# The middle row of a per-channel 7 by 7 convolution goes from VectorE to TensorE

## Chip, core and metric

The kernel runs on one core of a Trainium2 chip. The metric is the device time of one execution in microseconds (us); lower is better. Five engines run at the same time and wait for one another by semaphores: TensorE (PE in the rows, PEld for its weight loads) multiplies matrices, VectorE (DVE) and GpSimd (POOL) work elementwise, ScalarE (ACT) applies functions and copies, SyncE (SP) starts transfers.

## What is computed

16 images of 256 channels and 32 by 32 points pass through two layers. Both start with a group normalisation and add their result to their input.

```python
# layer A, one image x (256, 32, 32), xh = groupnorm(x)
key = softmax_over_points(K_w @ xh + K_b)                      # 49 x 1024
f   = xh @ key.T                                               # 256 x 49
w   = conv1_w @ relu(layernorm(conv0_w @ f + b0)) + b1         # 7 x 7 taps for each channel
x   = x + depthwise_conv7x7(xh, w)                             # each channel with its own 49 taps
...
# layer B: projections to 128 channels at three resolutions (1024, 256, 64 points),
# 16-state scans forwards and backwards over them, layernorm, upsampling, gate, projection
h = h * exp(delta * A) + delta * B * x ;  y += C * h
x = x + out_w @ (y * silu(z))
```

## The kernel before

A channel sits on a partition, so an image is 2 tiles (`CT`, index `t`) of 128 partitions by 1024 points. Three images are in flight: in one pass of `body(i, j, m)` image i is in the scans of layer B, image j in the convolution of layer A, and image m has its taps made (normalisation, softmax, the small matrices). `stages` writes that pass for each engine: 37 **units** (`NU`), then a **bridge** between two images. Every engine has its own order of instructions, written out by hand, and meets the others through counting semaphores only.

- There are five passes in the program text: one with image m alone, one with j and m (the **head**, in which no scan runs), a loop of 14 with all three, one with i and j (its units hold a convolution too, its bridge no work for an image m), one with i alone. Units with both scans and a convolution are thus run for 15 images, bridges with all three for 14; 13 of these jump back to the start of the loop (L1363).
- Units 0 to 4 hold the coarse levels of the scan, units 5 to 36 one state each at 1024 points. In such a unit VectorE runs `scan` (L553), `weigh` (L563, or L566 in the coarse units) and `inputs` of the unit after it (L531). TensorE spreads one row of B over 128 partitions into the PSUM tensor `slot_b` (`put_b`, L850) once the scan has freed it, and one row of C into `slot_c` (`put_c`) once `weigh` has. `inputs` of unit k+1 needs `put_b(k+1)`, and `weigh` overlaps it. ScalarE makes the decays (L1136), GpSimd adds each product to `y` (`gather`, L1268).
- Small steps for image m (`pre`, for example `gn_spread` in unit 6, `a_spread_` in 23, `a_f3_` in 25, `a_w_` in 26), the normalisations of y (`norm`) and `conv_add` stand between them on VectorE. I call them **fillers**; a scan waits behind them in VectorE's order.
- The convolution on TensorE: a tap is a matmul with a diagonal 128 by 128 matrix (`diag`) over the shifted image, in three float16 products and two halves, so 6 matmuls of 512 columns (L799, `taps`), all into `pconv`. `taps_at` deals the taps to the units 0 to 32 by the weights `ROOM`; in a unit they stand behind `put_c`. In the bridge 7 taps of the next image stand between other matmuls.
- The diagonals of a row of 7 taps are made on GpSimd by two instructions (`make_row`, L1245), in a ring of 4 rows; `row_unit` derives from `taps_at` in which unit a row is made, behind that unit's `gather`.
- Row 3 of 7, the **middle row**, is not on TensorE: `middle_taps` runs its 14 taps (7 of each of the two tiles) on VectorE in the bridge, one instruction a tap (L465 the first of a tile, which adds `xr`; L471 the others), into `xm`, which lies in `u`. The first 7 stand ahead of `chunk_first` (L494), the last 3 just ahead of `inputs(j, 0)`. `copy_x` (L1046) copies `xm` to `xn`, to which `conv_add` (L479) adds the TensorE part.

The bridge has a chain over three engines: TensorE's projection of image j (L807), its lower levels (L825), the first chunk (L839, L840), `chunk_first` on VectorE, the second chunk on TensorE, the normalisation of image i (L880, L886), taps, a projection (L816), the output of image i (L893), taps, `put_b(j, 0)`, and at last `inputs(j, 0)`.

Of the kernel before, what the change touches and what calls it, by code (L numbers as in the profile page):

```python
# [62 lines left out]
def build(nc, a, out):  # L63
    with ExitStack() as ctx:  # L64
# [79 lines left out]
        wmid = sb("wmid", [P, CT, KK])  # L144
# [22 lines left out]

        xm = u[:, 0:CT * HW].rearrange("p (t n) -> p t n", t=CT)
# [28 lines left out]
        ea_a, ea_b = Chain("dve_a", 19), Chain("dve_b", 3)  # L197
# [27 lines left out]
        mid_tap = Count("mid_tap", len(MID_TAPS))  # L225
# [110 lines left out]
        def _(dve):  # L336
# [106 lines left out]
            def a_w_(j):  # L443
# [177 lines left out]
            def bridge(i, j, m):  # L621
                def some(lo, hi):
                    if m is not None:
                        middle_taps(m, BRIDGE_MID[lo], BRIDGE_MID[hi])
# [793 lines left out]
```

## Time and profile before

| | us |
|---|---|
| median of 3 runs | 4960.43 (4957.82 to 4961.94) |
| the profiled execution | 4965.09 |
| its span, from the first to the last instruction | 4963.0 |
| VectorE busy | 4530.2 |
| TensorE matmuls busy | 3601.6 |
| GpSimd busy | 3041.7 |
| ScalarE busy | 1639.2 |

The mean granted TensorE clock was 0.852 of full speed. The spans of instructions on one engine may overlap slightly, since the next one starts while the last one drains.

### The profile page before, as it was taken

Reading aid. Unit: us, or ns where it says so; the run is one execution under the profiler, and the core shown is the slowest. Engines: PE = TensorE matmul, PEld = TensorE weight load, DVE = VectorE, ACT = ScalarE, POOL = GpSimd, SP = SyncE. Lnnn points to the kernel's source line nnn. Section 1 sums busy time; section 2 is a strip of 40 time slices with the busy share of each in tenths; the row PEclk is TensorE's granted clock in tenths of the full one; section 3 lists DMA queues with packets and bytes.
Section 4 is the critical chain, followed back from the end, with each engine's and each line's share of the span. In section 5 each row is a group of like instructions: output and inputs, shape, how many; then the busy total and the mean of one; then the engine's idle time right before and its main releaser. Section 6 shows DMA issues by size and latency. Waiting matters only on the chain. (4 is left out here: it accounts for less than half of the span.)

```text
span 4963.0 us, 44208 instructions
## 1 busy us (share of the span) xinstructions
PE 3601.6 (73%) x14156; PEld 1531.7 (31%) x14156; DVE 4530.2 (91%) x3880; ACT 1639.2 (33%) x2518; POOL 3041.7 (61%) x1748
## 2 busy tenths in 40 slices
PE   6877786777868777786777867778676777867744
PEld 3423332333323223332233323333232333322210
DVE  4499999999998999999999999999999999999898
ACT  1232334323333333333324233233333323342332
POOL 3375756757566575755757566575765757557474
PEclk8988888888988888888888888888888888888855
DMA  1000000000000000000000000000000000000000
GB/s 35 9 1 0 18 1 18 0 0 18 1 18 0 9 9 0 18 0 18 1 0 18 1 18 0 0 18 1 18 0 17 1 0 18 1 9 1 9 0 9
DMA packets 11799, 38.96 MB, mean 8 GB/s; under 512 B 1680, under 2 KB 2848, under 8 KB 11552
## 3 DMA queue, kind: packets, MB, share of 16 engines
q1 hardware_dynamic: 11552, 35.70, 2.0%
q8 instruction: 151, 2.47, 0.2%
q14 instruction: 96, 0.79, 0.1%
HBM read 18.92 MB, written 16.78 MB: 7 GB/s over the span
## 5 line engine op out<-in xcount | busy, mean ns | idle before, releaser
L799 PE MATMUL pconv<-pad,diag 128*128 128x512 f16 x8064 | 2114.1, 416 | 49.6 <-DVE xn L479 38.4
L1268 POOL TENSOR_TENSOR y<-y,work 128x1024 f32<-128x1024 f32 (+2 forms) x672 | 1332.6, 1983 | 1220.9 <-DVE work L563 1202.7
L1136 ACT ACTIVATE work<-delta,nega 128x1024 f32<-128x1024 f32 (+1 forms) x768 | 696.5, 931 | 2282.5 <-DVE work L553 2060.5
L799 PEld LDWEIGHTS pconv<-pad,diag 128*128 128x128 f16 x8064 | 835.7, 104 | 1225.2 <-issue 351.3
L553 DVE TENSOR_TENSOR_SCAN work<-work,slot_b 128x1024 f32<-128x1024 f32 x496 | 1132.0, 2282 | 23.2 <-issue 3.2
L850 PE MATMUL slot_b<-bcs,sel 96*128 96x512 bf16 (+2 forms) x1536 | 431.3, 388 | 782.4 <-DVE work L553 536.6
L531 DVE TENSOR_TENSOR slot_b<-slot_b,u 128x1024 f32<-128x1024 f32 x496 | 607.6, 1225 | 164.9 <-PE slot_b L850 145.3
L563 DVE TENSOR_TENSOR work<-slot_c,work 128x1024 f32<-128x1024 f32 x512 | 626.9, 1224 | 22.0 <-DVE work L553 0.5
L1263 POOL TENSOR_TENSOR work<-work 128x512 f32<-128x512 f32 (+3 forms) x384 | 549.4, 1431 | 134.7 <-DVE work L566 117.2
L850 PE MATMUL slot_c<-bcs,sel 96*128 96x512 bf16 (+2 forms) x1536 | 417.1, 376 | 292.2 <-DVE work L563 199.9
L1245 POOL TENSOR_TENSOR diag<-id,chi 128x896 f16<-128x896 f16 x192 | 378.9, 1974 | 248.1 <-DVE csc L384 180.0
L850 PEld LDWEIGHTS slot_b<-bcs,sel 96*128 96x128 bf16 x1536 | 108.7, 105 | 1036.2 <-DVE work L553 712.9
L553 DVE TENSOR_TENSOR_SCAN work<-work 128x1028 f32<-128x1028 f32 x144 | 393.2, 2730 | 2.0 <-POOL y L1268 0.2
L1245 POOL TENSOR_TENSOR diag<-id,clo 128x896 f16<-128x896 f16 x192 | 370.0, 1927 | 0.0
L471 DVE SCALAR_TENSOR_TENSOR u<-xh,wmid,u 128x992 f32<-128x992 f32 (+2 forms) x192 | 307.4, 1655 | 0.0
L850 PEld LDWEIGHTS slot_c<-bcs,sel 96*128 96x128 bf16 x1536 | 100.7, 101 | 607.0 <-DVE work L563 452.2
L1224 POOL TENSOR_TENSOR bcs<-rest,bcs 32x512 bf16<-32x512 f32 (+1 forms) x96 | 165.7, 1726 | 187.6 <-ACT bcs L1108 187.6
L566 DVE TENSOR_TENSOR work<-slot_c,work 128x1024 f32<-128x1024 f32 x160 | 195.0, 1219 | 7.8 <-PE slot_c L850 3.8
L1227 POOL TENSOR_TENSOR delta<-delta,rs 128x512 f32<-128x512 f32 (+1 forms) x96 | 99.0, 1031 | 102.0 <-DVE rs L509 102.0
L1231 POOL TENSOR_TENSOR u<-delta,f 128x512 f32<-128x512 f32 (+1 forms) x96 | 135.4, 1411 | 8.6 <-POOL delta L1227 2.2
L839 PE MATMUL pm<-f,wbc 128*96 128x512 f32 (+1 forms) x192 | 101.7, 616 | 37.0 <-DVE rest L494 29.8
L1093 ACT ACTIVATE bcs<-pm 96x512 bf16<-96x512 f32 (+1 forms) x96 | 46.9, 488 | 170.2 <-PE pm L839 170.2
(177 smaller groups left out, 3693.2 us busy)
## 6 DMA issues: line engine op xcount, KB each, us to landing
xr<-in_x SPq DMA_DIRECT2D x16, 1024.0 KB, 4.8
out<-ob SPq DMA_DIRECT2D x16, 1024.0 KB
w<-in_w SPq DMA_DIRECT2D x2, 256.0 KB
wc<-in_wc SPq DMA_DIRECT2D x2, 256.0 KB
wbc<-in_wbc SPq DMA_DIRECT2D x1, 144.0 KB
win<-in_win SPq DMA_DIRECT2D x1, 128.0 KB
wz<-in_wz SPq DMA_DIRECT2D x1, 128.0 KB
wo<-in_wo SPq DMA_DIRECT2D x1, 128.0 KB
```

What stands on the lines that cost most here:

```text
L471: ins = nc.vector.scalar_tensor_tensor(o, src, w, o, ALU.mult, ALU.add)
L531: nc.vector.tensor_tensor(o, i0, i1, ALU.mult).then_inc(u_bx.sem, 1)
L553: nc.vector.tensor_tensor_scan(hv, av, bv, 0.0, ALU.mult, ALU.add).then_inc(q_h.sem, 1)
L563: nc.vector.tensor_tensor(hv, slot_c[:, :], hv, ALU.mult).then_inc(q_pr.sem, 1)
L566: nc.vector.tensor_tensor(hv, slot_c[:, :].rearrange("p (m l) -> p m l", m=m), hv, ALU.mult).then_inc(q_pr.sem, 1)
L799: ins = nc.tensor.matmul(bank(pconv, k), w, pad[:, t, part, rows:rows + 16, dx:dx + W], start=first and m == 0, stop=last and m == 2)
L850: ins = nc.tensor.matmul(slot[:, o:o + per], sel[:, row0 + n0 + n:row0 + n0 + n + 1].to_broadcast([96, P]), bcs[:, so + c:so + c + per], s ...
L1136: ins = nc.scalar.activation(o, delta[:, so:so + ln], ACT.Exp, scale=nega[:, st, n0 + n:n0 + n + 1])
L1224: pool.tensor_tensor(bcs[0:32, s:s + n], rest[0:32, c % 2, 0:n], bcs[0:32, s:s + n], ALU.subtract).then_inc(ch_lo.sem, 1)
L1245: ins = pool.tensor_tensor(diag[:, r % RING, m, :, :], id16[:, None, :].to_broadcast([P, KK, P]), w[:, t, dy * KK:(dy + 1) * KK, None].to_ ...
L1263: pool.tensor_tensor(src[:, 0:m], src[:, 0:m], src[:, m:2 * m], ALU.add).then_inc(n_y.sem, 1)
L1268: pool.tensor_tensor(yv, yv, src[:, 0] if len(src.shape) == 3 else src, ALU.add).then_inc(q_y.sem, 1)
```

## The change

All 7 rows of both tiles are dealt to TensorE. `ROWS` has 14 rows in place of 12, so that TensorE has 98 taps an image in place of 84 and GpSimd makes 14 rows of diagonals in place of 12. `middle_taps`, its semaphore, the copy `wmid` in `a_w_` and the waits of ScalarE and GpSimd for `xm` are gone; `copy_x` reads `xr` itself. The 7 taps of TensorE in the bridge stay, so that its units get 89 in place of 75. One weight of `ROOM` goes from -28 to -27.

```diff
-MIDDLE = KK // 2
-ROWS = [(t, r) for t in range(CT) for r in range(KK) if r != MIDDLE]
+ROWS = [(t, r) for t in range(CT) for r in range(KK)]
-MID_TAPS = [(dx, t) for dx in sorted(range(KK), key=lambda d: abs(d - MIDDLE)) for t in range(CT)]
...
-                ch(nc.vector.tensor_copy(wmid[:, :, :], wg[:, :, MIDDLE * KK:(MIDDLE + 1) * KK]))
...
-            def middle_taps(j, lo, hi):
-                for n in range(lo, hi):
-                    dx, t = MID_TAPS[n]
-                    shift = dx - MIDDLE
-                    w = wmid[:, t, dx:dx + 1]
-                    if shift == 0:
-                        ins = nc.vector.scalar_tensor_tensor(xm[:, t, :], xh[:, t, :], w, xr[:, t, :], ALU.mult, ALU.add)
-                    else:
...
-                        ins = nc.vector.scalar_tensor_tensor(o, src, w, o, ALU.mult, ALU.add)
-                    ins.then_inc(mid_tap.sem, 1)
...
             def bridge(i, j, m):
-                def some(lo, hi):
-                    if m is not None:
-                        middle_taps(m, BRIDGE_MID[lo], BRIDGE_MID[hi])
-                some(0, 1)
...
-                act.wait_ge(mid_tap.sem, mid_tap.at(j + 1, 0))
-                nc.scalar.activation(xn[:, :, :], xm[:, :, :], ACT.Copy).then_inc(a_copy.sem, 1)
+                nc.scalar.activation(xn[:, :, :], xr[:, :, :], ACT.Copy).then_inc(a_copy.sem, 1)
...
-                if c == 2 and j is not None:
-                    pool.wait_ge(a_copy.sem, a_copy.at(j, 1))
...
-BRIDGE_MID = (0, 7, 10, 11, 11, 14)
...
-for k, v in {0: -16, 1: 8, 2: 4, 3: 14, 4: 4, 6: 6, 10: 0, 11: -8, 13: -10, 14: -8, 15: -28, 16: -10, 17: -12, 19: -4, 20: -10, 22: 3, 23: 7,
+for k, v in {0: -16, 1: 8, 2: 4, 3: 14, 4: 4, 6: 6, 10: 0, 11: -8, 13: -10, 14: -8, 15: -27, 16: -10, 17: -12, 19: -4, 20: -10, 22: 3, 23: 7,
```

The weights deal the taps anew. The units 0, 2, 3, 4, 6, 8, 10, 13, 16, 17, 19, 22, 24, 26, 27, 29 and 31 get one tap more, the units 14, 18 and 28 one fewer. Three places show what stands where. In these rows the line numbers of the changed kernel are its own: its L766 is L799 before, L817 is L850, L1209 is L1245, L1232 is L1268, L508 is L531.

VectorE at the end of the bridge of the loop, before, from the last output instruction to the jump back:

```order
L617 SCALAR_TENSOR_TENSOR ob<-slot_b,vec,xc 128x512
L468 REGISTER_ALU
L471 SCALAR_TENSOR_TENSOR u<-xh,wmid,u 128x32x29
L468 REGISTER_ALU
L471 SCALAR_TENSOR_TENSOR u<-xh,wmid,u 128x32x29
L468 REGISTER_ALU
L471 SCALAR_TENSOR_TENSOR u<-xh,wmid,u 128x32x29
L520 ISA
L531 TENSOR_TENSOR b<-slot_b,u 128x16x64
L1363 REGISTER_ALU
L1363 COMPARE_AND_BRANCH
```

And in the changed kernel:

```order
L594 SCALAR_TENSOR_TENSOR ob<-slot_b,vec,xc 128x512
L497 ISA
L508 TENSOR_TENSOR b<-slot_b,u 128x16x64
L1326 REGISTER_ALU
L1326 COMPARE_AND_BRANCH
```

Nothing stands between the output and `inputs(j, 0)` any more; the other 11 middle taps are gone from their places in the same way.

TensorE from `put_b(5)` in unit 3 to `put_b(6)` in unit 5, before:

```order
L850 MATMUL slot_b<-bcs,sel 128x512 x2
L786 REGISTER_ALU
L799 MATMUL pconv<-pad,diag 128x512 x12
L865 REGISTER_ALU
L850 MATMUL slot_c<-bcs,sel 128x256 x4
L799 MATMUL pconv<-pad,diag 128x512 x30
L865 REGISTER_ALU
L850 MATMUL slot_c<-bcs,sel 128x512 x2
L786 REGISTER_ALU
L799 MATMUL pconv<-pad,diag 128x512 x12
L858 REGISTER_ALU
L850 MATMUL slot_b<-bcs,sel 128x512 x2
```

And in the changed kernel:

```order
L817 MATMUL slot_b<-bcs,sel 128x512 x2
L766 MATMUL pconv<-pad,diag 128x512 x12
L832 REGISTER_ALU
L817 MATMUL slot_c<-bcs,sel 128x256 x4
L766 MATMUL pconv<-pad,diag 128x512 x18
L753 REGISTER_ALU
L766 MATMUL pconv<-pad,diag 128x512 x18
L832 REGISTER_ALU
L817 MATMUL slot_c<-bcs,sel 128x512 x2
L766 MATMUL pconv<-pad,diag 128x512 x18
L825 REGISTER_ALU
L817 MATMUL slot_b<-bcs,sel 128x512 x2
```

Between the same two spreads stand 66 matmuls of the convolution in place of 54, which is two taps more.

GpSimd in the units 23 to 27, before; L1268 is the `gather` of a unit, the pair of L1245 one row of diagonals:

```order
L1268 TENSOR_TENSOR y<-y,work 128x1024
L1257 REGISTER_ALU
L1268 TENSOR_TENSOR y<-y,work 128x1024
L1241 REGISTER_ALU
L1245 TENSOR_TENSOR diag<-id,chi 128x896
L1245 TENSOR_TENSOR diag<-id,clo 128x896
L1257 REGISTER_ALU
L1268 TENSOR_TENSOR y<-y,work 128x1024
L1257 REGISTER_ALU
L1268 TENSOR_TENSOR y<-y,work 128x1024
```

And in the changed kernel, units 23 to 26:

```order
L1232 TENSOR_TENSOR y<-y,work 128x1024
L1205 REGISTER_ALU
L1209 TENSOR_TENSOR diag<-id,chi 128x896
L1209 TENSOR_TENSOR diag<-id,clo 128x896
L1221 REGISTER_ALU
L1232 TENSOR_TENSOR y<-y,work 128x1024
L1221 REGISTER_ALU
L1232 TENSOR_TENSOR y<-y,work 128x1024
L1221 REGISTER_ALU
L1232 TENSOR_TENSOR y<-y,work 128x1024
L1205 REGISTER_ALU
L1209 TENSOR_TENSOR diag<-id,chi 128x896
```

A row stood behind the `gather` of unit 24; now one stands behind that of 23 and one behind that of 26. In the loop's units the rows were made in 5, 6, 8, 12, 17, 21 and 24, and are made in 5, 6, 7, 9, 12, 17, 20, 23 and 26.

## Rows read from the trace of the kernel before

**Rows 1.** The page: busy time by engine; the group of L471.

```profile
PE 3601.6 (73%) x14156; PEld 1531.7 (31%) x14156; DVE 4530.2 (91%) x3880; ACT 1639.2 (33%) x2518; POOL 3041.7 (61%) x1748
...
L471 DVE SCALAR_TENSOR_TENSOR u<-xh,wmid,u 128x992 f32<-128x992 f32 (+2 forms) x192 | 307.4, 1655 | 0.0
```

**Rows 2.** Timeline of VectorE, one bridge: start, length, instruction [idle before, releaser].

```profile
1102.74 4.00 DVE L465 SCALAR_TENSOR_TENSOR u<-xh,wmid,xr 128x1024 f32<-128x1024 f32 x2
...
1118.84 0.69 DVE L590 TENSOR_TENSOR delta<-slot_b,delta 128x512 f32<-128x512 f32 x1 [0.54 <-ACT delta L1158]
...
1135.54 1.21 DVE L531 TENSOR_TENSOR b<-slot_b,u 128x1024 f32<-128x1024 f32 x1
1137.92 2.32 DVE L553 TENSOR_TENSOR_SCAN work<-a,b 128x1040 f32<-128x1040 f32 x1 [1.17 <-issue]
```

**Rows 3.** Timeline of TensorE, the same bridge.

```profile
1114.83 0.67 PE L839 MATMUL pm<-f,wbc 128*96 128x256 f32 x2 [1.97 <-DVE rest L494]
...
1132.97 0.63 PE L850 MATMUL slot_c<-bcs,sel 96*128 96x64 bf16 x16
1138.01 1.03 PE L850 MATMUL slot_b<-bcs,sel 96*128 96x256 bf16 x4 [4.41 <-issue]
```

**Rows 4.** Timeline of TensorE, the head of the program.

```profile
64.21 45.15 PE L799 MATMUL pconv<-pad,diag 128*128 128x512 f16 x192 [7.96 <-POOL diag L1245]
...
174.52 18.80 PE L799 MATMUL pconv<-pad,diag 128*128 128x512 f16 x84
```

**Rows 5.** Timeline of TensorE, units 3 to 5, 20 and 24.

```profile
1181.39 1.03 PE L850 MATMUL slot_b<-bcs,sel 96*128 96x512 bf16 x2 [8.23 <-POOL bcs L1224]
...
1186.86 6.81 PE L799 MATMUL pconv<-pad,diag 128*128 128x512 f16 x30
...
1196.62 0.59 PE L850 MATMUL slot_b<-bcs,sel 96*128 96x512 bf16 x2
...
1296.78 5.06 PE L799 MATMUL pconv<-pad,diag 128*128 128x512 f16 x12
...
1325.81 0.61 PE L850 MATMUL slot_b<-bcs,sel 96*128 96x512 bf16 x2 [0.23 <-DVE work L553]
```

**Rows 6.** Timeline of VectorE: `inputs` that waited for `slot_b`, in the units 5, 8, 15, 21.

```profile
1197.25 1.23 DVE L531 TENSOR_TENSOR slot_b<-slot_b,u 128x1024 f32<-128x1024 f32 x1 [0.75 <-PE slot_b L850]
...
1218.62 1.23 DVE L531 TENSOR_TENSOR slot_b<-slot_b,u 128x1024 f32<-128x1024 f32 x1 [0.59 <-PE slot_b L850]
...
1263.26 1.23 DVE L531 TENSOR_TENSOR slot_b<-slot_b,u 128x1024 f32<-128x1024 f32 x1 [1.49 <-PE slot_b L850]
...
1305.82 1.23 DVE L531 TENSOR_TENSOR slot_b<-slot_b,u 128x1024 f32<-128x1024 f32 x1 [4.86 <-PE slot_b L850]
```

**Rows 7.** Timeline of VectorE: small fillers, at the start and in units 6, 23, 25, 26, 34.

```profile
20.38 0.17 DVE L368 TENSOR_TENSOR sa<-sa 128x8 f32<-128x8 f32 x1
...
1204.40 2.14 DVE L367 TENSOR_TENSOR sa<-sa 128x8 f32<-128x8 f32 x1
...
1318.39 0.16 DVE L427 SCALAR_TENSOR_TENSOR sa<-sa 128x2 f32<-128x2 f32 x1
...
1328.06 2.27 DVE L438 TENSOR_SCALAR f<-f,sa 128x98 f32<-128x98 f32 x1
...
1336.15 0.94 DVE L449 COPY wmid<-wg 128x14 f32<-128x14 f32 x1
...
1386.96 1.60 DVE L368 TENSOR_TENSOR sg<-sg 128x8 f32<-128x8 f32 x1
```

**Rows 8.** Timeline of GpSimd, units 23, 24, 26 and 34.

```profile
1315.99 2.35 POOL L1268 TENSOR_TENSOR y<-y,work 128x1024 f32<-128x1024 f32 x1 [2.88 <-DVE work L563]
...
1324.64 1.69 POOL L1245 TENSOR_TENSOR diag<-id,chi 128x896 f16<-128x896 f16 x1
...
1334.71 2.35 POOL L1268 TENSOR_TENSOR y<-y,work 128x1024 f32<-128x1024 f32 x1 [4.44 <-DVE work L563]
...
1386.86 1.68 POOL L1245 TENSOR_TENSOR diag<-id,chi 128x896 f16<-128x896 f16 x1
```

More of the change, by code:

```diff
@@ L143, in build @@
         whi = sb("whi", [P, CT, K2], F16)
-        wmid = sb("wmid", [P, CT, KK])
         wlo = sb("wlo", [P, CT, K2], F16)
@@ L166, in build @@
         u = sb("u", [P, LS])
-        xm = u[:, 0:CT * HW].rearrange("p (t n) -> p t n", t=CT)
         y = sb("y", [P, 2, LF])
@@ L196, in build @@
         ob_ready = Count("ob_ready", 1)
-        ea_a, ea_b = Chain("dve_a", 19), Chain("dve_b", 3)
+        ea_a, ea_b = Chain("dve_a", 18), Chain("dve_b", 3)
         act_a, act_b = Chain("act_a", 2), Chain("act_b", 1)
@@ L224, in build @@
         c_w = Count("c_w", 1)
-        mid_tap = Count("mid_tap", len(MID_TAPS))
         a_copy = Count("a_copy", 1)
@@ L457, in a_w_ @@
                 ch.end()
-            def middle_taps(j, lo, hi):
-                for n in range(lo, hi):
-                    dx, t = MID_TAPS[n]
-                    shift = dx - MIDDLE
-                    w = wmid[:, t, dx:dx + 1]
-                    if shift == 0:
-                        ins = nc.vector.scalar_tensor_tensor(xm[:, t, :], xh[:, t, :], w, xr[:, t, :], ALU.mult, ALU.add)
-                    else:
-                        dve.wait_ge(mid_tap.sem, mid_tap.at(j, n - CT + 1))
-                        o = img(xm[:, t, :], W)[:, :, max(0, -shift):W - max(0, shift)]
-                        src = img(xh[:, t, :], W)[:, :, max(0, shift):W - max(0, -shift)]
-                        ins = nc.vector.scalar_tensor_tensor(o, src, w, o, ALU.mult, ALU.add)
-                    ins.then_inc(mid_tap.sem, 1)
             def conv_add(j, t):
@@ L630, in bridge @@
                     chunk_first(j, 0)
-                some(1, 2)
                 if i is not None:
@@ L640, in bridge @@
                     chunk_last(j, 1)
-                some(2, 3)
                 if i is not None:
                     output(i, 0)
-                    some(3, 4)
                     output(i, 1)
-                else:
-                    some(3, 4)
-                some(4, 5)
                 if j is not None:
```

## The prediction

> **What bounds the kernel now.** I read the page first. VectorE is busy 91% of the span, TensorE 73%, GpSimd 61% [rows 1]. That makes VectorE the first suspect and says that removing 14 of its instructions an image should pay. But an average says nothing of single places, so I then read the timelines of VectorE, TensorE and GpSimd over one whole image. In most fine units VectorE has no gap: the scan, `weigh` and `inputs` follow one another, and TensorE waits for the scan. In the bridge the middle taps fill VectorE without a gap, yet `put_b(j, 0)`, which VectorE's last step there needs, is made by TensorE. In the units with a slot wait [rows 6] TensorE is the one that is late, and VectorE stands. So in the loop the bound changes from place to place, and in the head of the program, where no scan runs, TensorE alone sets the time: 192 matmuls in 45.15 us and, later, 84 without a break in 18.80 us [rows 4].
>
> **Head.** The convolution of image 0 runs with no VectorE work to hide behind, and it gets 14 taps more, which are 84 matmuls. A row of just 84 of them took 18.80 us [rows 4]. That is the cost, less some 0.8 us (an estimate: the diagonals of the first row, for which TensorE waited 7.96 us [rows 4], are made with less VectorE work beside them). Term: **+18**, from 17 to 19. The bridge behind the head I cost at nothing, as VectorE there waits for TensorE.
>
> **Bridge, 14 times.** The 14 middle taps go. Their busy time is 307.4 us for the 192 counted [rows 1] and 4.00 for a pair of first ones [rows 2], so 19.2 + 4.0 = 23.2 us an image. This is not the gain. From 1102.74 to the second scan's start at 1137.92 [rows 2] VectorE serves a chain that is TensorE's for the most part. What the taps cost that chain is one place: the 7 taps ahead of `chunk_first` (L494) made it late, and TensorE stood 1.97 us for it ahead of the second chunk [rows 3]. With the taps gone all behind it moves 2.0 us earlier: the normalisation at 1118.84 [rows 2], which waited for ScalarE alone, the output, and `put_b(j, 0)`. The last 3 taps then held `inputs(j, 0)` until 1135.54 [rows 2], though `put_b(j, 0)` was done at about 1133.1, as `put_c(0)` runs behind it from 1132.97 [rows 3]. This would be another 2.4 us. But the jump back to the loop's start lies behind it. TensorE did nothing for 4.41 us there, released by nothing that the profile shows, and only then made `put_b(1)` (1138.01, 1.03 us) [rows 3]. This gap counts from its own last matmul, so it moves by 2.0 and not by 4.4. VectorE shows a remainder of 1.17 us of the same kind [rows 2]; the middle taps in its queue may have hidden the rest. If VectorE needs a gap of TensorE's size after it has issued `inputs(j, 0)`, its first scan also moves by just 2.0 us; if it needs none, unit 1's `inputs` waits for `put_b(1)` and gains at most 1137.92 + 2.32 = 1140.24 less 1137.07, or 3.1 us. I take 2.0, since VectorE's 1.17 lies at the same instant as TensorE's end of gap. 13 of the bridges jump; the last falls through and gains 2.0 + 2.4. Term: 13 x 2.0 + 4.4 = **-30**, bounds -45 and -30.
> The Trainium skill (Advanced Engine Details and Errata, Control Flow Timing) gives a compare-and-branch about 108 ns. By it the whole 4.4 us would be gained 14 times, 62 us, and the sum below would end 32 us lower. The row with 4.41 us of idle time speaks against it, and the measurement decides.
>
> **Units, 15 images.** A tap is 18.80 / 14 = 1.34 us of TensorE at full clock [rows 4]. `weigh` hides about 0.5 us of a late `put_b` (1.22 us of `weigh`, of which `put_b` itself takes 0.61 [rows 5]), so an added tap costs 1.3 us less the gap ahead of the next `put_b` and less 0.5. Place by place:
> - Units 3 to 5: from 1181.39 to 1196.62 [rows 5] TensorE is busy without a gap, and VectorE already waits 0.75 us for the result at 1197.25 [rows 6]. The two added taps stand wholly ahead of it: **+2.6**. Nothing hides them.
> - Unit 8: wait of 0.59 [rows 6]. It comes with matmuls at half the granted clock after TensorE stood for `gn_spread`; one more tap shortens that idle time: **-0.6**.
> - Unit 15: wait of 1.49 [rows 6]; unit 14 has one tap fewer in front of it: **-1.4**.
> - Unit 21: wait of 4.86 [rows 6]. Ahead of it 12 matmuls took 5.06 us [rows 5], against 18.80 x 12 / 84 = 2.7 at full clock. If the added tap of unit 19 keeps the clock up, 2.4 us come back; if not, none. I take **-1.4**.
> - Units 22, 24, 29, 31 have small gaps, such as 0.23 us ahead of `put_b(26)` [rows 5]: at worst 1.3 - 0.23 - 0.5 = 0.6 each. Units 17 and 18 trade a tap across a place where the clock is low, and unit 10 has its `gather` delayed by a row that is now made in unit 9. Together I take **+2.3**, bounds -0.4 and +4.5.
>
> The other part is GpSimd. A small VectorE step takes 0.17 us where GpSimd is silent, and 1.60 us where a row of diagonals starts 0.1 us before it (1386.86 against 1386.96) [rows 7, 8]: it ends just when the diagonal instruction of 1.68 us does. So a filler made of short dependent steps pays about 1.5 us for each of the two instructions of a row beside it. The Trainium skill (SBUF — State Buffer, Who interferes with whom) says it as a rule: a VectorE instruction with two SBUF inputs and a GpSimd one that reads SBUF exclude each other for the whole instruction. The trace agrees (0.17 against 1.60 us), and the sum is the same by either. It speaks against this change because of where the added rows land:
> - Unit 23: `gather` runs 1315.99 to 1318.34 [rows 8], and L427 at 1318.39 took 0.16 us [rows 7], as no row followed. Now one does. L427 waits for its first, L428 for its second instruction: **+3.0**.
> - Unit 26: L449 waited for the `gather` there (0.94 us [rows 7]). It is gone, -1.0, but L454, L455 and L456, short steps too, now stand beside a row: waits of 1.3 and 1.6, **+1.9** net.
> - Unit 25: the row of unit 24 (1324.64 [rows 8]) delayed the `gather` for which L438 waited 2.27 us [rows 7]. The row has moved: **-0.7**.
> - Unit 6: L367 waited 2.14 us [rows 7] for a `gather` that row 5 delayed. As VectorE now comes 2.6 us later than TensorE let it before, most of this wait is gone, while L514 ahead of it collides newly: **-1.2**.
>
> Sum of an image: 2.6 - 0.6 - 1.4 - 1.4 + 2.3 + 3.0 + 1.9 - 0.7 - 1.2 = +4.5. All nine are not independent: 3 us more in unit 23 and 1.9 in unit 26 give TensorE time in which its added taps of units 22 to 27 hide, so I take 0.7 off: **+3.8**, x 15 = **+57**. `copy_x` with its other source costs nothing, as ScalarE is a third busy [rows 1].
>
> **Sum.** 18 - 30 + 57 = +45 us. The profiled execution took 4965.1, with 2.1 of it outside the span; it would take 5010. It stands 4.7 above the median of the runs, so the median becomes 4960.4 + 45 = **5005 us**, 0.9% slower. Break-even is at (30 - 18) / 15 = 0.8 us an image in the units.
>
> **Rivals.**
> - The clock holds (faster). TensorE gets 16% more convolution in its units, and the gaps after which it fell to 1.2 GHz shrink. The Trainium skill (TensorE: Matmul & The Clock Gate, The HAM clock gate) has activity release the clock. If it holds at 2.4 GHz from unit 3 on, then the stretch 1181.39 to 1186.86 loses 1.8 us, unit 21 another 1.0, the low place of unit 17 1.0 and that of unit 10 0.5: 3.8 - 4.3 = -0.5 an image, 18 - 30 - 8 = -20, **4940**. It decides once it is worth over 3 us an image. Against it: the 8.23 us idle time ahead of 1181.39 [rows 5] is hardly touched. Chance 0.08.
> - GpSimd's rows don't collide. Without +3.0, +1.9, -0.7, -1.2 and unit 10's part of 0.9 the units cost about 0.5, so -4 us in all: **4956**, no change. Against it stand the 1.60 us [rows 7]. Chance 0.13.
> - VectorE is the bound everywhere, and the filler was not hidden by anything. Then 14 x 23.2 = 325 us go, less the head: **4655**. Against it are 1.97 and 4.41 us of TensorE's own [rows 3]. Half of it would still be clearly faster. Chance 0.03.
> - Everything adds up: the clock stays low in units 17 and 21 and each small gap costs its worst, +7.5 an image, so 18 - 30 + 112 = +100, **5060**. Chance 0.12.
> - My forecast, 4978 to 5045 us: 0.64.
>
> **How the numbers follow.** The bounds are the bridge's 15 us, the small gaps' -0.4 to +4.5 an image and the clock's 1.4. The range of 4955 to 5048 takes in the forecast and the case without collisions, and leaves out the two ends. A measurement of this kernel can tell about 0.2% (10 us) from no change. Faster by more: 0.08 + 0.03 + a bit of the second rival, 0.13. Within: 0.12. Slower: 0.75.
>
> **What would show it.** In the changed profile: TensorE's convolution of image 0 is 18 us longer; the wait of the second chunk (L839 before) for VectorE is gone from the bridge, but the idle time of over 4 us at the loop's start stays; `inputs(6)` waits some 3 us for `slot_b`; L427, L428 and the last steps of `a_w_` take 1.5 us each beside a row; the wait in unit 15 is nearly gone. It is wrong if the bridge gains over 4 us, if those steps stay at 0.2 us, or if the wait ahead of unit 6 is short since TensorE's clock is full.

## The result, and the profile after

The changed kernel takes **5037.37 us**, median of 3 runs (5035.14 to 5038.66), against 4960.43 before. The ratio is 1.0155, 95% interval 1.0132 to 1.0178: 77 us or 1.5% slower. The profiled span is 5035.6 us, the mean granted TensorE clock 0.867.

The page after, busy time by engine and the group of `inputs` (busy, mean ns of one | idle time before them and what ended most of it):

```profile
PE 3852.9 (77%) x15500; PEld 1643.0 (33%) x15500; DVE 4195.6 (83%) x3640; ACT 1636.9 (33%) x2518; POOL 3076.9 (61%) x1812
...
L508 DVE TENSOR_TENSOR slot_b<-slot_b,u 128x1024 f32<-128x1024 f32 x496 | 608.1, 1226 | 213.2 <-PE slot_b L817 194.2
```

VectorE has 335 us less work than in [rows 1] and the program is longer: little of what it lost lay on the path. To see where time went I compared the start of every one of the 42 scans of every image in the two traces; the growth from one scan to the next belongs to the unit between. The first scan of image 0 starts 20.5 us later; the 15 bridges behind it give back 34.8 us in all; the units add 88.0 us. Together 73.7, against 72.6 in the spans. All per-unit numbers below are medians over the 14 images of the loop, read in this way, unless they say otherwise.

**Bridge.** VectorE in the bridge of the changed kernel (start, length, instruction, [idle before, releaser]), answering to [rows 2]:

```profile
1152.80 0.69 DVE L567 TENSOR_TENSOR delta<-slot_b,delta 128x512 f32<-128x512 f32 x1 [4.29 <-ACT delta L1124]
...
1167.14 1.22 DVE L508 TENSOR_TENSOR b<-slot_b,u 128x1024 f32<-128x1024 f32 x1 [3.69 <-PE slot_b L817]
1170.37 2.33 DVE L530 TENSOR_TENSOR_SCAN work<-a,b 128x1040 f32<-128x1040 f32 x1 [2.01 <-issue]
```

TensorE in the same bridge, answering to [rows 3]:

```profile
1148.88 0.59 PE L806 MATMUL pm<-f,wbc 128*96 128x256 f32 x2
...
1170.53 0.61 PE L817 MATMUL slot_b<-bcs,sel 96*128 96x256 bf16 x4 [2.97 <-issue]
```

The 1.97 us of TensorE ahead of the second chunk are gone. Where VectorE ran middle taps it now stands: 4.29 us for ScalarE, 3.69 us for `put_b(j, 0)`, and 2.01 us at the loop's jump. TensorE's idle time at the jump, 4.41 us in [rows 3], is 2.97. VectorE's 1.17 us of [rows 2] was not the rule: over the 13 jumps of the kernel before, it stood 0.68 to 1.17 us at seven and 0.10 us at the other six; in the changed kernel it stands 1.81 to 2.19 us at all of them.

**Head.** TensorE in the head, answering to [rows 4]:

```profile
188.61 22.76 PE L766 MATMUL pconv<-pad,diag 128*128 128x512 f16 x102
...
224.45 5.05 PE L766 MATMUL pconv<-pad,diag 128*128 128x512 f16 x12 [3.29 <-DVE sg L367]
...
241.31 4.89 PE L766 MATMUL pconv<-pad,diag 128*128 128x512 f16 x18
```

102 matmuls in 22.76 us are the 0.22 us each of [rows 4]. The last two rows took 4.16 and 4.21 us before.

**Units 23 to 28.** VectorE, answering to [rows 7]. L421 and L422 are L427 and L428 of before, L446 and L447 are L454 and L455:

```profile
1348.70 0.92 DVE L420 TENSOR_TENSOR sa<-sa 128x2 f32<-128x2 f32 x1
1349.66 1.60 DVE L421 SCALAR_TENSOR_TENSOR sa<-sa 128x2 f32<-128x2 f32 x1
1351.29 1.61 DVE L422 SCALAR_TENSOR_TENSOR sa<-sa 128x2 f32<-128x2 f32 x1
...
1364.28 1.23 DVE L508 TENSOR_TENSOR slot_b<-slot_b,u 128x1024 f32<-128x1024 f32 x1 [3.15 <-PE slot_b L817]
1365.42 0.33 DVE L432 TENSOR_SCALAR f<-f,sa 128x98 f32<-128x98 f32 x1
...
1372.54 0.17 DVE L445 RECIPROCAL sa<-wsc 128x2 f32<-128x2 f32 x1
1372.74 1.50 DVE L446 TENSOR_TENSOR wg<-wg,sa 128x98 f32<-128x98 f32 x1
1374.27 1.57 DVE L447 CAST whi<-wg 128x98 f16<-128x98 f32 x1
...
1385.73 1.23 DVE L508 TENSOR_TENSOR slot_b<-slot_b,u 128x1024 f32<-128x1024 f32 x1 [1.36 <-PE slot_b L817]
```

GpSimd beside it, answering to [rows 8]:

```profile
1349.56 1.68 POOL L1209 TENSOR_TENSOR diag<-id,chi 128x896 f16<-128x896 f16 x1
1351.20 1.68 POOL L1209 TENSOR_TENSOR diag<-id,clo 128x896 f16<-128x896 f16 x1
...
1372.44 1.68 POOL L1209 TENSOR_TENSOR diag<-id,chi 128x896 f16<-128x896 f16 x1
1374.08 1.70 POOL L1209 TENSOR_TENSOR diag<-id,clo 128x896 f16<-128x896 f16 x1
```

Each of the four steps begins 0.1 to 0.3 us after a row's instruction and ends with it. What I had not foreseen stands on TensorE in the same stretch:

```profile
1352.95 0.38 PE L741 MATMUL pm<-sa,ones 128*128 128x2 f32 x2 [1.15 <-DVE sa L422]
1355.15 0.72 PE L817 MATMUL slot_b<-bcs,sel 96*128 96x512 bf16 x2 [1.81 <-DVE work L530]
...
1357.24 6.57 PE L766 MATMUL pconv<-pad,diag 128*128 128x512 f16 x18
...
1378.39 0.60 PE L817 MATMUL slot_b<-bcs,sel 96*128 96x512 bf16 x2 [2.42 <-DVE work L530]
...
1380.48 3.92 PE L766 MATMUL pconv<-pad,diag 128*128 128x512 f16 x12
```

TensorE waits for the late step L422, then for the late scan, and then its 18 matmuls take 6.57 us, where 4.1 is the full-clock time. `put_b(26)` is late by that, and VectorE stands 3.15 us (1364.28). Three units on the same follows the second collision: 2.42 us idle, 12 matmuls in 3.92 us, 1.36 us of VectorE.

**Units 5 and 8.** VectorE, answering to [rows 6]:

```profile
1232.93 1.23 DVE L508 TENSOR_TENSOR slot_b<-slot_b,u 128x1024 f32<-128x1024 f32 x1 [3.17 <-PE slot_b L817]
...
1254.26 1.23 DVE L508 TENSOR_TENSOR slot_b<-slot_b,u 128x1024 f32<-128x1024 f32 x1 [1.81 <-PE slot_b L817]
```

The first was foreseen. The second is the wait of 0.59 us of [rows 6], which I had taken for shrinking: it has grown to 1.81.

### The profile page after: what moved, and what is told of

Same layout as the page of the kernel before. It is cut to its first block and busy times, and to the rows that moved or that the text cites. A ratio compares the mean times of both kernels' runs of the same rounds, so it can differ in the third digit from the quotient of the medians.

```text
span 5035.6 us, 46565 instructions
## 1 busy us (share of the span) xinstructions
PE 3852.9 (77%) x15500; PEld 1643.0 (33%) x15500; DVE 4195.6 (83%) x3640; ACT 1636.9 (33%) x2518; POOL 3076.9 (61%) x1812
## 5 line engine op out<-in xcount | busy, mean ns | idle before, releaser
L766 PE MATMUL pconv<-pad,diag 128*128 128x512 f16 x9408 | 2439.7, 415 | 62.5 <-POOL diag L1209 32.7
L1232 POOL TENSOR_TENSOR y<-y,work 128x1024 f32<-128x1024 f32 (+2 forms) x672 | 1313.7, 1955 | 1228.4 <-DVE work L540 1212.0
L766 PEld LDWEIGHTS pconv<-pad,diag 128*128 128x128 f16 x9408 | 970.8, 104 | 1433.2 <-issue 393.1
L817 PE MATMUL slot_b<-bcs,sel 96*128 96x512 bf16 (+2 forms) x1536 | 411.1, 373 | 699.4 <-DVE work L530 489.5
L508 DVE TENSOR_TENSOR slot_b<-slot_b,u 128x1024 f32<-128x1024 f32 x496 | 608.1, 1226 | 213.2 <-PE slot_b L817 194.2
L1209 POOL TENSOR_TENSOR diag<-id,chi 128x896 f16<-128x896 f16 x224 | 428.0, 1911 | 284.4 <-DVE csc L378 173.0
L817 PE MATMUL slot_c<-bcs,sel 96*128 96x512 bf16 (+2 forms) x1536 | 409.9, 371 | 244.8 <-DVE work L540 170.0
L817 PEld LDWEIGHTS slot_b<-bcs,sel 96*128 96x128 bf16 x1536 | 110.0, 104 | 927.6 <-DVE work L530 643.8
L1209 POOL TENSOR_TENSOR diag<-id,clo 128x896 f16<-128x896 f16 x224 | 392.6, 1753 | 0.0
L817 PEld LDWEIGHTS slot_c<-bcs,sel 96*128 96x128 bf16 x1536 | 101.2, 100 | 539.3 <-DVE work L540 402.3
L1190 POOL TENSOR_TENSOR bcs<-rest,bcs 32x512 bf16<-32x512 f32 (+1 forms) x96 | 152.6, 1590 | 189.5 <-ACT bcs L1074 189.5
L471 DVE TENSOR_TENSOR rest<-pm,bcs 64x512 f32<-64x512 f32 (+1 forms) x96 | 53.0, 552 | 147.8 <-ACT bcs L1059 147.8
L484 DVE TENSOR_TENSOR rs<-qs,rs 128x512 f32<-128x512 f32 (+1 forms) x96 | 114.4, 1192 | 0.0
```

What stands on the lines that cost most here:

```text
L508: nc.vector.tensor_tensor(o, i0, i1, ALU.mult).then_inc(u_bx.sem, 1)
L766: ins = nc.tensor.matmul(bank(pconv, k), w, pad[:, t, part, rows:rows + 16, dx:dx + W], start=first and m == 0, stop=last and m == 2)
L817: ins = nc.tensor.matmul(slot[:, o:o + per], sel[:, row0 + n0 + n:row0 + n0 + n + 1].to_broadcast([96, P]), bcs[:, so + c:so + c + per], s ...
L1190: pool.tensor_tensor(bcs[0:32, s:s + n], rest[0:32, c % 2, 0:n], bcs[0:32, s:s + n], ALU.subtract).then_inc(ch_lo.sem, 1)
L1209: ins = pool.tensor_tensor(diag[:, r % RING, m, :, :], id16[:, None, :].to_broadcast([P, KK, P]), w[:, t, dy * KK:(dy + 1) * KK, None].to_ ...
L1232: pool.tensor_tensor(yv, yv, src[:, 0] if len(src.shape) == 3 else src, ALU.add).then_inc(q_y.sem, 1)
```

## The experiments

Ratios are to the kernel before, run beside each kernel; its medians in the four sets were 4958.2, 4963.8, 4959.0 and 4958.7 us. Comparisons with the changed kernel use its 5037.4 us, beside which the kernel before took 4960.4; a difference of 5 us between two sets is no more than these medians differ, and only the scans can tell it.

### What the two rows of diagonals cost

My theory after the result: the collisions of units 23 and 26 cost what was forecast, and the clock after them is a second price. The rival: the time is TensorE's added taps, wherever it shows. Three kernels tell them apart.

```diff
                 for m, w in enumerate((chi, clo)):
+                    if r in (12, 13):
+                        ins = pool.tensor_tensor(diag[:, r % RING, m, 0:1, 0:8], id16[:, None, 0:8],
+                                                 w[:, t, 0:1, None].to_broadcast([P, 1, 8]), ALU.mult)
+                        continue
```

> The changed kernel in which the four GpSimd instructions of the last two rows of diagonals (rows 12 and 13, made in units 23 and 26) write 8 elements in place of 896. The matmuls on these rows stay, on old diagonals, so all of TensorE's work is kept and the values of the last two rows of the convolution are left out. Theory: beside these rows the short VectorE steps pay +3.0 (unit 23) and +1.9 us (unit 26) an image, and because TensorE stands for the late steps its granted clock falls, which costs a further 2.0 (unit 25) and 1.4 us (unit 28). All of it goes: 5.0 to 8.3 us an image, 15 times, 75 to 125 us, so 4912 to 4962 us. Rival, TensorE's added taps are the price wherever it shows up: at most 1 us an image, so 5022 us or more, and the wait behind the 18 matmuls of unit 25 stays over 2.5 us.

Measured: **4888.6 us** (4887.9 to 4889.6), ratio 0.9858 (0.9842 to 0.9875). That is 149 us less than the changed kernel and outside both ranges. Unit 23 gives back 2.9, unit 26 2.6, unit 25 2.1, unit 28 1.5 us, as the theory has it, and unit 8, in most images, another 1.6. The bridges together are 9.5 us shorter; by what step stays open. The head is 5.6 us shorter. Of this 3.4 us are there before either of the two rows is made: GpSimd's first row begins at 56.01 us in place of 58.40, and the 216 matmuls behind it take 49.41 us in place of 50.46. Most of the rest are two groups of matmuls at the end of the head at a higher clock, 4.49 and 4.21 us in place of 5.05 and 4.89; why it is higher is open. VectorE and TensorE there:

```profile
1313.71 0.16 DVE L421 SCALAR_TENSOR_TENSOR sa<-sa 128x2 f32<-128x2 f32 x1
...
1332.11 0.21 DVE L447 CAST whi<-wg 128x98 f16<-128x98 f32 x1
```

```profile
1318.06 4.14 PE L766 MATMUL pconv<-pad,diag 128*128 128x512 f16 x18
```

The rival is ruled out: with all its taps TensorE makes a kernel 1.4% faster than before once these two rows are nearly free.

```diff
+LATE = {12: 24, 13: 27}
...
 def row_unit(r):
+    if r in LATE:
+        return LATE[r]
```

> The changed kernel with row 12 made in unit 24 in place of 23 and row 13 in unit 27 in place of 26; nothing is left out. Theory: the collisions hang on the unit alone. Units 23 and 26 lose +3.0 and +1.9; in unit 24 the row delays the gather for which the next filler waits, some +1.5 back. With the clock's part of 0 to 3.4 the gain is 3.4 to 6.8 us an image, 50 to 100 us, so 4937 to 4987 us. Rival, a collision only moves to the next filler: within 1 us an image, 5022 to 5052 us.

Measured: **4935.45 us** (4934.2 to 4936.3), ratio 0.9952 (0.9935 to 0.9969): 102 us off, just beyond the theory's end, and faster than before. Units 23, 26 and 28 give back 2.9, 2.6 and 1.5 us. Unit 25 gives 1.3 in place of 2.1, since its first filler again waits for the delayed gather (1.85 us in place of 0.33), and unit 27 loses 1.2.

```diff
...
+                if j is not None and k in (23, 26):
+                    for n in range(2):
+                        done = 2 * (k == 26) + n
+                        if done or not (isinstance(j, int) and j == 0):
+                            pool.wait_ge(spared.sem, spared.at(j, done))
+                        pool.tensor_tensor(spare[:, :, :], id16[:, None, :].to_broadcast([P, KK, P]),
+                                           id16[:, 0:KK, None].to_broadcast([P, KK, P]), ALU.mult).then_inc(spared.sem, 1)
```

> The kernel before, with two more GpSimd instructions of the size of a row's (128 x 896, into a tile that nothing reads) behind the gather in units 23 and 26; TensorE and VectorE do just what they did. Theory: the port alone makes the loss of those units, +3.0 and +1.9 us an image, and 0 to 2 more where TensorE then stands: 4.9 to 7 us, 15 times, so 5033 to 5065 us. Rival, the rows hurt only together with TensorE's added taps: under 2 us an image, 4990 us or less.

Measured: **5024.5 us** (5017.8 to 5034.2), ratio 1.0138 (1.0120 to 1.0156): 66 us for four GpSimd instructions an image that nothing reads. That is short of the theory's 5033 to 5065, but far from the rival. Unit 26 lost 2.5 us, unit 23 only 1.4, and of the second price unit 28 shows 1.6 us in five of the images and unit 25 nothing. VectorE in unit 23, and GpSimd:

```profile
1326.99 1.60 DVE L429 SCALAR_TENSOR_TENSOR sa<-sa 128x2 f32<-128x2 f32 x1
1328.62 0.16 DVE L430 SCALAR_TENSOR_TENSOR sa<-sa 128x2 f32<-128x2 f32 x1
```

```profile
1326.89 3.44 POOL L1303 TENSOR_TENSOR spare<-id 128x896 f16<-128x896 f16 x2
```

Here the second of the pair waits for the semaphore of the first; two of them take 3.44 us, where a row's second begins 1.64 us after its first. It starts at 1328.65, just after L430 and not before it, and L430 pays nothing. A step that starts first goes free; one that starts second waits for what is left of GpSimd's instruction: 1.60 us of a row's, and 0.92 us where the `gather` was already under way (L420 above). So a tenth of a microsecond can decide between nothing and 1.4 us.

### Is it the clock?

TensorE's idle time behind a late filler is filled with matmuls that nobody reads; the fillers stay late.

```diff
+            def fill(n):
+                for _ in range(n):
+                    nc.tensor.matmul(bank(pm, 1), id16[:, :], pad[:, 0, 0, 0:16, 0:W], start=True, stop=True)
...
             def a_sum4(j):
+                fill(5)
...
                     if UNITS[k][0] == 1:
+                        if j is not None and k in (24, 27):
+                            fill(8)
```

> The changed kernel with matmuls that compute nothing used (0.22 us each, into a bank of pm that is free there) put into the idle time of TensorE behind the collisions: 5 in unit 23 (idle 1.15 us), 8 ahead of put_b(25) in unit 24 (idle 1.81) and 8 ahead of put_b(28) in unit 27 (idle 2.42). The collisions themselves stay. Theory: it is the idle time that lets the granted clock fall (0.78 and 0.73 in units 24 and 25, 0.85 and 0.84 in 27 and 28), and the low clock that makes the waits of 3.15 us (unit 25) and 1.36 us (unit 28). Filled, the clock stays at 1.00, unit 25 gives back 2.1 and unit 28 1.4 us, 15 times: -3.5 x 15 = -53, 4984 us (4975 to 4995). Rival A, the clock falls whatever TensorE does there: 21 more matmuls are 4.6 us an image of work, at least some of it on the path, so 5037 us or more. Rival B, only one of the two places comes back: 5003 to 5020 us.

Measured: **4986.6 us** (4986.2 to 4987.9), ratio 1.0053 (1.0037 to 1.0070). With 21 more matmuls an image the kernel is 51 us faster. Unit 25 gives back 2.1 and unit 28 1.5 us. Next to nothing moves elsewhere, but for the last image with a convolution: it has no late filler, and there the added matmuls cost 3.1 us. The stretches of units 23, 24 and 25 in the changed kernel and in this one (window, its length, busy us and count of TensorE, its weight loads, VectorE, ScalarE, GpSimd, then TensorE's granted clock, share and GB/s of the DMA):

```profile
1343.67:1352.85 9.18, 8.06 (x38) 3.33 (x35) 8.99 (x10) 1.15 (x1) 6.31 (x4) 1.00 0.00 0
1352.85:1357.61 4.76, 2.30 (x7) 0.84 (x8) 4.69 (x6) 1.17 (x2) 1.21 (x2) 0.78 0.00 0
1357.61:1366.52 8.91, 8.91 (x31) 3.46 (x30) 5.62 (x8) 1.62 (x3) 3.52 (x2) 0.73 0.00 0
```

```profile
1329.24:1338.42 9.18, 9.04 (x44) 3.92 (x42) 8.99 (x9) 1.15 (x1) 5.94 (x4) 1.00 0.00 0
1338.42:1343.18 4.76, 4.04 (x19) 1.44 (x19) 4.70 (x5) 1.54 (x3) 1.57 (x1) 1.00 0.02 3
1343.18:1349.98 6.80, 6.80 (x32) 2.97 (x31) 6.33 (x8) 1.25 (x2) 3.13 (x2) 1.00 0.00 0
```

Unit 23 is 9.18 us long in both, so the collision is the same. TensorE was busy 2.30 of 4.76 us in unit 24 in the one, 4.04 in the other, and unit 25 takes 8.91 against 6.80. So TensorE's idle time, through the clock that it lets fall, is shown to be the cause of the two later waits. The Trainium skill (TensorE: Matmul & The Clock Gate, The HAM clock gate) has activity release the clock; the trace agrees, 1.00 with the idle time filled and 0.73 without.

### The two taps ahead of `put_b(6)`

```diff
+EARLIER = {3: 2, 4: 1}
...
     n = min(n, PREP)
-    return BRIDGE_TAPS[-1] + -(-(TAPS - BRIDGE_TAPS[-1]) * sum(ROOM[:n]) // sum(ROOM[:PREP]))
+    return EARLIER.get(n, 0) + BRIDGE_TAPS[-1] + -(-(TAPS - BRIDGE_TAPS[-1]) * sum(ROOM[:n]) // sum(ROOM[:PREP]))
```

> The changed kernel with two taps taken from units 3 and 4 (one each) and made in unit 2, ahead of whose end TensorE stands idle; nothing is left out. Theory: the two taps that the change puts ahead of put_b(6) are its +2.6 to +3.0 us an image, and in unit 2 they lie in idle time: -2.6 an image, -39 us, so 4998 us (4992 to 5005). Rival, unit 6 is late because TensorE's clock is low when it begins with unit 3, whatever the number of taps: within 0.7 us an image, 5027 us or more, or the clock stays up from unit 2 on and more than 3.5 us an image come back, under 4985 us.

Measured: **5011.4 us** (5002.6 to 5020.6), ratio 1.0105 (1.0085 to 1.0124), 26 us off where 39 were expected. Unit 5 gives back 2.7 us as forecast, but unit 6 takes 1.5. TensorE and VectorE there:

```profile
1228.20 2.74 PE L766 MATMUL pconv<-pad,diag 128*128 128x512 f16 x6 [4.37 <-POOL diag L1209]
```

```profile
1222.14 1.23 DVE L508 TENSOR_TENSOR slot_b<-slot_b,u 128x1024 f32<-128x1024 f32 x1 [1.22 <-PE slot_b L817]
...
1231.77 1.23 DVE L508 TENSOR_TENSOR slot_b<-slot_b,u 128x1024 f32<-128x1024 f32 x1 [4.76 <-PE slot_b L817]
```

TensorE reaches tap 35 earlier and stands 4.37 us for the diagonals of row 5, which GpSimd makes in unit 5 as before. One wait has become another. Unit 8 gives 1.6 us in most images, and in half of them unit 21 takes 1.7. The time lies between the theory and its first rival.

With this and the moved rows together:

> The changed kernel with both moves: row 12 in unit 24 and row 13 in unit 27, and one tap each of units 3 and 4 in unit 2. The moved rows alone took 102 us off, the moved taps 26 us, of which a part was the clock in units 8, 25 and 28 that the moved rows bring back too. Theory: the gain of unit 6 less what unit 7 loses is 1.2 us, the clock of unit 8 1.1 us an image, and they add to that of the rows: -2.3 x 15 = -34, so 4901 us, at least 4890 to 4915. Rival, the two gains are the same time twice: 4925 us or more.

Measured: **4927.8 us** (4925.6 to 4930.8), ratio 0.9930 (0.9914 to 0.9947). The number is the rival's, 8 us below the moved rows alone and not 34, but its cause isn't. Beside the moved rows the two gains that the theory counted did come: unit 5 gives 2.6 us and unit 6 takes 1.3, and unit 8 gives 1.7. They were lost in places that neither named: unit 11 loses 1.2 us in most images and unit 18, in 9 of them, 1.9 to 2.0, while unit 27 gives 1.2.

### The bridge

```diff
-ROWS = [(t, r) for t in range(CT) for r in range(KK)]
+ROWS = [(t, r) for t in range(CT) for r in range(KK) if r != KK // 2]
```

This is against the changed kernel, with the weight of `ROOM` back at -28.

> The kernel before without the 14 middle taps: the middle row of the convolution is left out (no VectorE taps, no matmuls, no diagonals; the copy of its weights goes too), and all else is in the places of before. It measures the bridge alone. Theory: the taps cost the bridges 2.0 to 2.8 us each, 14 times, 28 to 39 us, and the copy of the weights, which waits beside the gather in unit 26, 0.7 to 1.0 us an image, 10 to 15 us: 4904 to 4920 us. Rival A, nothing hid the taps: 14 x 23.2 = 325 us, 4635 us. Rival B, the idle time at the loop's start takes everything back: 4940 us or more.

Measured: **4914.6 us** (4908.5 to 4920.6), ratio 0.9904 (0.9887 to 0.9920). The theory holds. The bridges give back 1.6 to 2.6 us each in the loop, 4.3 in the last, and unit 26 0.8 us an image. Leaving the middle row out altogether is worth 49 us. Of the 325 us of VectorE's taps the bridges show 32.9, so some nine tenths were hidden.

```diff
+from concourse.bass import OrderedEngineSet
...
-    with eng.Fori(0, B - 2) as i:
+    with eng.bass.Fori(0, B - 2, engines=OrderedEngineSet([eng.engine]), hint_back_edge=True) as i:
```

> The changed kernel with a prefetch hint for the jump at the end of the loop, on every engine that runs it; no work is changed. In the changed kernel TensorE stands 2.97 and VectorE 2.01 us at each of the 13 jumps, released by nothing that the profile shows. Theory: this is the fetching of the first instructions of the loop, and with the hint most of it goes, 2.0 to 3.0 us a jump, 26 to 39 us: 4996 to 5010 us, and the two idle times are under 1 us. Rival A, the time goes into the branch and the registers whatever is fetched: within 4 us of the changed kernel. Rival B, TensorE's gap closes, but VectorE waits for ScalarE or GpSimd there: under 1 us a jump, 5022 to 5035 us.

Measured: **5032.6 us** (5031.5 to 5034.4), ratio 1.0142 (1.0125 to 1.0159): 5 us off in place of 26 to 39. Yet the idle time is gone. VectorE, then TensorE, at the jump:

```profile
1163.42 1.23 DVE L508 TENSOR_TENSOR b<-slot_b,u 128x1024 f32<-128x1024 f32 x1 [3.69 <-PE slot_b L817]
1164.75 2.33 DVE L530 TENSOR_TENSOR_SCAN work<-a,b 128x1040 f32<-128x1040 f32 x1
```

```profile
1164.70 0.61 PE L817 MATMUL slot_b<-bcs,sel 96*128 96x256 bf16 x4 [0.85 <-DVE b L508]
...
1305.93 0.60 PE L817 MATMUL slot_b<-bcs,sel 96*128 96x512 bf16 x2 [2.58 <-DVE work L530]
...
1324.90 4.32 PE L766 MATMUL pconv<-pad,diag 128*128 128x512 f16 x12
```

The branch is still there and only the hint is new, so the gap was not the branch; that it was the fetching of the loop's first instructions follows from what the hint asks for. Each of the 13 bridges is 1.7 to 2.1 us shorter. The gain is given back in unit 21, +1.7 us in 13 images: the 12 matmuls at 1324.90 took 4.32 us, 2.84 in the changed kernel. From 1307.82 to there TensorE has the same work in both traces, and stands 0.65 us at most at a time. But ahead of that the traces differ. The 12 matmuls of unit 16 take 5.16 us in the changed kernel and 2.85 with the hint; then TensorE stands 2.58 us for the scan (1305.93), and the 12 of unit 17 take 4.26 us in place of 2.84. So the stretches at the low clock already lie elsewhere ahead of unit 21; why it falls there is open.

```diff
-    with eng.Fori(0, B - 2) as i:
+    with eng.Fori(0, B - 2, 2) as i:
         body(i, i + 1, i + 2)
+        body(i + 1, i + 2, i + 3)
```

> The changed kernel with two images in each pass of the loop, so that 6 jumps stay of 13; no work is changed. Theory: a jump costs 2.0 to 3.0 us, a plain passage from one image to the next almost nothing: 7 x 2.0 to 3.0 = 14 to 21 us, 5014 to 5021 us. Rival: a program this long stands at every passage as it does at the jump, since nothing has fetched it either: within 5 us of the changed kernel.

Measured: **5034.5 us** (5032.8 to 5041.1), ratio 1.0148 (1.0131 to 1.0165). By its total the rival would be right, and it is not: the 7 passages that no longer jump are 1.7 to 2.2 us shorter each, and in the 7 images behind them unit 21 takes 1.7 us more, as with the hint.

The hint again, in the kernel before:

> The kernel before with the prefetch hint for the jump at the loop's end; no work is changed. Theory of the bridge: TensorE's 4.41 us at the jump shrink to about 1, but VectorE is held by its last middle taps and has just 1.17 us of its own to lose, so the first scan moves by 1.1 to 2.0 us at 13 jumps: 14 to 26 us, 4935 to 4947 us. Rival A, the middle taps hid the jump altogether: 4955 us or more. Rival B, TensorE's whole gap counted, 3.4 x 13 = 44 us: 4916 us or less.

Measured: **4963.9 us** (4962.4 to 4965.6), ratio 1.0010 (1.0000 to 1.0019): rival A. TensorE and VectorE at the jump:

```profile
1134.68 1.21 DVE L531 TENSOR_TENSOR b<-slot_b,u 128x1024 f32<-128x1024 f32 x1
1135.95 0.61 PE L850 MATMUL slot_b<-bcs,sel 96*128 96x256 bf16 x4 [3.21 <-DVE b L531]
1136.00 2.33 DVE L553 TENSOR_TENSOR_SCAN work<-a,b 128x1040 f32<-128x1040 f32 x1
```

TensorE's gap is shorter, but VectorE is busy with middle taps up to 1134.68, and the bridges gain 0.6 to 1.1 us in every other image and nothing in the rest, 5.9 us in all, which the units take back. Of TensorE's gap 3.21 us are left, and now they are a wait for VectorE's `inputs`, which the last middle taps held. So most of the 4.41 us in [rows 3] was that wait as well, and not the jump: `put_b(1)` came 1.26 us after the end of `inputs`. In the kernel before, the middle taps were, in effect, what VectorE did while the instructions were fetched.

### A version that beats both

The moved rows, the moved taps and the hint in one kernel:

> The version with both moves and the prefetch hint. Theory: the hint takes 1.8 us off each of the 13 bridges here too, 23 us, so 4905 us. In the changed kernel it brought a slower clock in unit 21, +1.7 us an image, which ate the gain. Rival: that is so here too, 4922 to 4935 us. Either is faster than the kernel before by over 0.5%.

Measured: **4891.9 us** (4890.8 to 4892.5), ratio 0.9862 (0.9845 to 0.9878), 1.4% faster than before, 36 us below the same without the hint and 13 below the theory. Here the 13 bridges give back 1.2 to 3.3 us each, and the units take nothing back on the whole (they are 5.0 us shorter), though unit 21 still loses 1.2 to 1.7 us in four images.

Against that version, one more row moves:

```diff
-LATE = {12: 24, 13: 27}
+LATE = {5: 4, 12: 24, 13: 27}
```

> The version with both moves and the hint, and row 5 made at the end of unit 4 in place of unit 5, ahead of that unit's gather. In the version without it TensorE, now earlier at tap 35, stands 3.99 us for the diagonals of row 5, and inputs(7) waits 4.24 us for put_b(7) behind it: this is where most of what the moved taps gained was given back. Theory: the row starts 2.35 us earlier (one gather), both waits shrink by that: -2.3 us an image, 15 times, 35 us: 4857 us (4850 to 4870). Rival A, TensorE's granted clock gives it back elsewhere, as in the run with the hint alone: 4880 us or more. Rival B, the gather that is now behind the row holds a later scan: over 4892 us.

Measured: **4877.3 us** (4871.6 to 4881.2, 5 runs), ratio 0.9833 (0.9818 to 0.9848). It is 15 us better, not 35, between the theory and its rival A. VectorE:

```profile
1208.92 1.23 DVE L508 TENSOR_TENSOR slot_b<-slot_b,u 128x1024 f32<-128x1024 f32 x1 [2.23 <-PE slot_b L817]
...
1211.57 1.46 DVE L361 TENSOR_TENSOR sa<-sa 128x8 f32<-128x8 f32 x1
1213.06 1.60 DVE L362 TENSOR_TENSOR sa<-sa 128x8 f32<-128x8 f32 x1
```

The wait went from 4.24 to 2.23 us as expected. But VectorE now comes to `gn_spread` while row 6 is being made, and its two steps pay 1.46 and 1.60 us where they took 0.17 each (the first in all images of the loop, the second in most): what the earlier row gave, the next collision takes. The bridges are 5.9 us longer in all.

## Why the prediction was right in sign and short in size

The direction, and the time inside the range, came out by the mechanism that was named: a cheap gain in the bridge, smaller than the head, the taps ahead of `put_b(6)` and the collisions together. 45 us were forecast, 77 measured. Part of the size agrees by luck, as errors of both signs below cancel. By its steps:

| step | forecast, us | found, us | by |
|---|---|---|---|
| head | +18 | +20.5 | scan of image 0 |
| bridges | -30 | -34.8 | scans; 4914.6 with the row left out |
| unit 5 (units 3 to 5) | +2.6 | +2.9 | scans; 2.7 back with the taps moved |
| unit 6 | -1.2 | -1.0 | scans |
| unit 8 | -0.6 | +0.8 | scans |
| unit 15 | -1.4 | -1.3 | scans |
| unit 21 | -1.4 | -2.7 | scans |
| unit 23 | +3.0 | +2.9 | scans; 2.9 back with the row moved |
| unit 25 | -0.7 | +1.3 | scans; 2.1 back with TensorE filled |
| unit 26 | +1.9 | +1.8 | scans |
| unit 28 | nothing | +1.5 | scans; 1.5 back with TensorE filled |
| small gaps | +2.3 | -0.5 | units 9, 10, 11 and 18 |
| an image | +3.8 | +5.4 to 6.2; 4.7 in the first, 9.4 and 9.5 in two, 1.0 in the fifteenth | scans |

- **Head.** The 84 matmuls cost their 18 us, less the start earlier by 0.6 (0.8 was the estimate). The 12 and the 18 further on ran at a lower clock, 5.05 and 4.89 us against 4.16 and 4.21 before; that is most of the 2.5 us above the forecast.
- **Bridge.** The size was right, and the main reading: the 1.97 us went, and the time at the jump was not gained. One premise and one of the signs were wrong. TensorE's gap was said to count from its own last matmul and to stay over 4 us; it is 2.97, since most of the 4.41 had been the wait for `inputs` behind the middle taps (3.21 with the hint in the kernel before). That 2.0 us a jump came out all the same is in part luck: it is 2.0 to 2.1 where VectorE had not stood at the jump before, and 2.5 to 3.0 where it had. The cause of the gap, which was left open, goes with the hint. The Trainium skill (Advanced Engine Details and Errata, Control Flow Timing) has about 108 ns for the branch. The traces do not speak against that for the branch alone, since with the hint the scan follows at 1164.75 after 0.10 us, as it does where nothing jumps; without the hint the jump takes 2 to 3 us. VectorE's gap was 1.17 us in [rows 2] and is 2.01 now, so the taps had hidden part of it, as the prediction held possible.
- **Collisions.** The three sizes were right within 0.2 us. The step that failed is the one behind them: "3 us more in unit 23 and 1.9 in unit 26 give TensorE time in which its added taps [...] hide, so I take 0.7 off". TensorE can't use that time, since its next `put_b` needs the late scan and its sums the late filler. It stands, 1.15 and 1.81 us, then 2.42 us, the granted clock falls from 1.00 to 0.73, and two more waits come out of it, 2.1 and 1.5 us. The term should have been +3.6 and was -0.7. Of these 4.3 us the small gaps, priced 2.8 too high, covered a part; what is left is most of the difference to +3.8 an image. The 14 images of the loop are 2.4 us each above the forecast, the fifteenth is 2.8 below it, and that makes the 31 us that the units are off. The fifteenth has no image m and so no late filler; the prediction multiplied the collisions by 15 where they come 14 times.
- **Unit 8.** The rule used, that one more tap shortens the idle time, was wrong by 1.4 us. TensorE still stood 1.84 us for the scan behind `gn_spread`, whose steps collide, and 12 matmuls took 5.01 us.
- **Unit 21.** Here the clock stayed up, the 12 matmuls took 2.84 us in place of 5.06, and all 2.7 us came, beyond the 2.4 that the prediction gave as the most. That the added tap did it is not shown: with the hint the same taps are there, and the 12 matmuls take 4.32 us.
- **Small gaps.** Forecast at +2.3, they came to -0.5: none cost its worst, and unit 11 gave 1.2 back. The errors of units 8 and 21 cancel.

Of the rivals, "the rows don't collide" was wrong, and more instructive than I took it for. It gave 4956; with only two rows all but free the kernel takes 4888.6. Made nearly free, the two rows give back 149 us, of which at least the 3.4 at the start of the head are not theirs, and made one unit later 102. The prediction had (3.0 + 1.9) x 15 = 74 for them. So what decided the sign was not the move of the middle row but where two of its rows are made. A slip without effect: the 16% more convolution in TensorE's units, named with the rival on the clock, is 19%, 89 taps for 75.

## What to carry to other kernels

A helper engine's instructions can hold up those of another (1.60 us in place of 0.16 here), and the price hangs on what stands beside them. Put rows of diagonals beside instructions such as `weigh` and `inputs`, which have an operand in PSUM: in the kernel before, they took their usual 1.22 us each beside the row of unit 24 (L563 at 1325.79, L531 at 1326.93). Keep the rows away from chains of short dependent steps, and look again after every edit that shifts the phase. When a step on one engine gets later, ask what the others do meanwhile: if TensorE stands, its clock is the second bill, here 3.6 us an image on top of 4.7. When a total doesn't move, compare the starts of a repeated landmark in both traces before you call a mechanism wrong: with the hint and with two bodies a loop the gain was there and was lost 160 us later.

## What the runs showed that I had not expected

- 21 matmuls an image that nothing reads made the kernel 51 us faster (5037.4 to 4986.6), by keeping the granted clock at 1.00 behind the late fillers (units 23 to 25 above).
- The idle time at a loop's jump, 2.0 us on VectorE and 3.0 on TensorE in the changed kernel, is gone from VectorE with a prefetch hint, and 0.85 us that wait for VectorE remain on TensorE.
- L447, a cast with one operand in SBUF, took 1.57 us beside a row and 0.21 without one. L445, a reciprocal with one operand, took 0.17 us although a row had begun 0.1 us before it. One operand is no safeguard by itself.
- The clock of unit 21 fell with the hint although TensorE had stood 0.65 us at most at a time in the 17 us ahead of it. The traces differ further ahead (2.58 us at 1305.93), but no run shows that this is the cause.
